# Causal and full attention heads on one core: other shapes of the head loads and of the bias path, a compact band, and zero-weight matmuls

## The chip, the core and the metric

The program runs on one core of one Trainium2 chip. The metric is the device time of one execution, in microseconds (us). Before the change three runs took 5108.78, 5110.0 and 5099.33 us (median 5108.78).

## What is computed

The input `x` is 2 x 2048 x 256, float32. It goes through two layers, each an attention and a feed-forward part:

```
x += attn0(LN(x))    16 heads of 16, all 2048 keys: softmax(q k^T) v, then Wff and a bias
x += moe(LN(x))      6 experts, top 2, and a shared one (also ahead of attn0: "macaron")
x += 0.5 * lstm(LN(x))
x += attn1(LN(x))    16 heads of 16, causal, rotary q and k, and a relative-position term:
                     scores[q,k] += q . rel[clip(k - q, -32, 32) + 32]
                     ctx[q]      += sum_k attn[q,k] rel[clip(k - q, -32, 32) + 32]
x += 0.5 * lstm(LN(x))
```

With two batches each attention has 32 heads (`NH`). In the causal one every key more than 32 back shares one row of `rel`, which is folded into the values. Only a band of 32 keys (`REL`) before each query needs a score term and an output term of its own.

## The kernel before, in words

The stages are, in order: `moe_stage` 0, `qkv_full_stage`, `heads_full_stage`, `project_full_stage`, `moe_stage` 1, `lstm_stage`, `qkv_causal_stage`, `heads_causal_stage`, `project_causal_stage`, `lstm_stage`. Each writes out one program per engine, and semaphores alone tie them together. SP issues nearly all transfers, in the order written, and a wait on SP holds back all behind it.

**Heads, both kinds.** q and k of a head lie in SBUF as 48 rows (high and low parts of float32r, 16 each) at partition 0 and again at 64, in a ring of four heads (`load`, L1126 to L1129 and L1495 to L1498). A 49th row of q is minus the row maximum (`row_load`, L1511), so that the score matmul (L1198, L1608) gives what exp takes. While PE scores head i, it also computes the maxima of heads i+1 and i+2 (`far`, L1226, L1659, L1665), and DVE reduces them. The order is written out in `body`: a causal head has 8 steps (`NSTEP`), each a pair of key tiles with five score matmuls, three `far` units, the bias added by matmuls with the identity (`bias`, L1619, L1622), and the weighted values (L1638) into bank 7. After the fifth step PE turns the maxima of head i+1 into a row (`row`, L1671), ACT copies it (L1740), and SP writes it into q of head i+1. The first score matmul of head i+1, in the last step of head i, waits for that.

**Bias path.** `qkv_causal_stage` leaves the 32 band scores of each query in DRAM (`rel_scores`, `k.TD`). `fill_bias_tiles` (called in `moe_stage` 1) has filled the array `bias_tiles` (`k.BB`) with 512 copies of a masked 128 x 160 tile. `skew(i)` (L1489) writes the 32 scores of each query over them, DRAM to DRAM, in runs of 128 bytes at a pitch of 161 numbers. Read back at a pitch of 160, each row is shifted by one more, which makes the diagonal band (`causal_bias`, L1502).

**Band path.** DVE adds the bias to the scores of the band, takes the maximum and leaves the sums in SBUF (L1794). POOL stores them to DRAM (`store_band`, L1571, `k.PB`). `project_causal_stage` reads the 32 band scores of each query back (`band`, L2002), in runs of 128 bytes.

**SP in a causal head** (`body` in `heads_causal_stage`): `load(i+3)`, which ends in the bias load and in `skew(i+4)`, then `store(i-1)`, then `row_load(i+1)`.

## Time and profile before

| | |
|---|---|
| three runs | 5108.78, 5110.0, 5099.33 us |
| the profiled execution | 5106.48 us, its span 5104.8 us, mean granted clock 0.888 |
| PE busy | 4455.2 us (87%) |
| DVE busy | 2996.9 us (59%) |
| ACT busy | 2297.0 us (45%) |
| POOL busy | 648.1 us (13%) |
| full heads, first load issued to last matmul | 640 to 2155 us |
| causal heads, first `skew` issued to last output copy | 3140 to 4728 us |
| projection of the causal heads | 4728 to 4873 us |

An engine's busy time is the sum of its instructions. The granted clock is TensorE's share of full speed: 1.00 is 2.4 GHz, 0.50 is 1.2 GHz. In a row of the timeline the first number is the start in us from the start of the span, the second the length. What stands in brackets is how long the engine was idle before, and what ended that. SPq is the queue of the sync engine.

### The profile page before, as it was taken

How to read it: one execution, taken by the hardware profiler on the slowest of the kernel's cores; microseconds unless marked ns; L12 is line 12 of the kernel's file. 1: busy time of each engine (PE TensorE's matmuls, PEld its weight loads, DVE VectorE, ACT ScalarE, POOL GpSimd, SP SyncE). 2: the span in 40 equal slices, each digit the busy share in tenths (PEclk: the TensorE clock that was granted, in tenths of full speed). 3: DMA queues.
4: the chain of work that ended last, by engine and by line, in shares of the span. 5: the costliest groups of instructions: out<-in, count | busy, mean ns of one | idle time of the engine just before them, and what ended most of it. 6: DMA issues, size and time to landing. Idle time of an engine off the chain costs nothing. (4 is left out here: it accounts for less than half of the span.)

```text
span 5104.8 us, 80050 instructions
## 1 busy us (share of the span) xinstructions
PE 4455.2 (87%) x25680; PEld 2625.2 (51%) x25680; DVE 2996.9 (59%) x5384; ACT 2297.0 (45%) x4375; POOL 648.1 (13%) x666
## 2 busy tenths in 40 slices
PE   7999859999999999889998965688978978889488
PEld 6888723333333333258886544345545545555355
DVE  6655668888888888456664355444444544444342
ACT  3222327777777777612222222334434434445222
POOL 2322100000000000013332024111111111111000
PEclk9999969999999999889999987778778878789699
DMA  2000311111111111039000026444444444341801
GB/s 77 0 0 1 138 50 42 42 39 41 37 37 42 42 38 33 11 113 296 0 0 18 0 86 183 112 93 93 103 95 95 105 94 96 97 98 44 133 26 33
DMA packets 316682, 343.08 MB, mean 67 GB/s; under 512 B 161280, under 2 KB 266760, under 8 KB 302600
## 3 DMA queue, kind: packets, MB, share of 16 engines
q1 hardware_dynamic: 299912, 296.20, 22.1%
q0 software_dynamic: 16384, 41.96, 2.9%
q8 instruction: 214, 3.51, 0.3%
q14 instruction: 172, 1.41, 0.1%
HBM read 239.26 MB, written 148.11 MB: 76 GB/s over the span
## 5 line engine op out<-in xcount | busy, mean ns | idle before, releaser
L1322 DVE TENSOR_REDUCE full_tops<-psum 128x1 f32<-128x1024 f32 x1024 | 1207.2, 1220 | 247.8 <-PE psum L1226 247.4
L1279 ACT ACTIVATE full_probs<-psum 128x512 f32<-128x512 f32 x2048 | 1067.2, 602 | 338.5 <-PE psum L1198 306.4
L1736 ACT ACTIVATE causal_probs<-psum 128x512 f32<-128x512 f32 (+3 forms) x1280 | 644.3, 533 | 761.2 <-PE psum L1622 389.4
L1784 DVE TENSOR_REDUCE causal_tops<-psum 128x1 f32<-128x1024 f32 (+7 forms) x704 | 587.4, 859 | 261.5 <-PE psum L1659 261.5
L1198 PE MATMUL psum<-full_q,full_k 49*128 49x512 f32 x2048 | 657.8, 482 | 49.5 <-ACT full_probs L1279 33.3
L1608 PE MATMUL psum<-causal_q,causal_k 49*128 49x512 f32 (+3 forms) x1280 | 465.3, 508 | 181.2 <-DMA causal_q<-causal_rows 171.0
L1198 PEld LDWEIGHTS psum<-full_q,full_k 49*128 49x128 f32 x2048 | 290.1, 189 | 640.4 <-ACT full_probs L1279 585.4
L1207 PE MATMUL psum<-full_probs,full_vh 128*32 128x512 f32 x4096 | 565.3, 625 | 0.7 <-ACT full_probs L1279 0.7
L1226 PE MATMUL psum<-full_k,full_q 48*128 48x512 f32 x2048 | 408.9, 463 | 64.7 <-DMA full_k<-qk_split 38.3
L1659 PE MATMUL psum<-causal_k,causal_q 48*128 48x512 f32 (+4 forms) x1152 | 375.2, 468 | 88.9 <-DMA causal_k<-rot_parts 46.9
L1638 PE MATMUL psum<-causal_probs,causal_vh 128*32 128x384 f32 (+3 forms) x3712 | 409.1, 501 | 1.2 <-ACT causal_probs L1736 1.2
L276 POOL TENSOR_TENSOR moe_h_lo<-moe_h,moe_h_hi 128x512 fp32r<-128x512 f32 x224 | 290.7, 1298 | 664.0 <-ACT moe_h_hi L389 664.0
L1608 PEld LDWEIGHTS psum<-causal_q,causal_k 49*128 49x128 f32 x1280 | 198.7, 212 | 320.7 <-DMA causal_q<-causal_rows 153.4
L313 PE MATMUL psum<-moe_x_hi,moe_w_hi 128*128 128x512 f32 x896 | 353.2, 394 | 3.9 <-DVE moe_h L455 3.8
L313 PE MATMUL psum<-moe_x_lo,moe_w_hi 128*128 128x512 f32 x896 | 350.9, 392 | 0.0
L313 PE MATMUL psum<-moe_x_hi,moe_w_lo 128*128 128x512 f32 x896 | 349.8, 390 | 0.0
L1794 DVE CUSTOM_DVE_ANT_0 xn<-psum,causal_bias 128x160 f32<-128x160 f32 (+1 forms) x384 | 107.5, 317 | 378.6 <-issue 378.6
L451 DVE TENSOR_TENSOR moe_ts<-psum,moe_sg 128x512 f32<-128x512 f32 x224 | 154.8, 691 | 296.8 <-ACT moe_sg L397 296.5
L1226 PEld LDWEIGHTS psum<-full_k,full_q 48*128 48x128 f32 x2048 | 203.8, 195 | 217.6 <-DVE full_tops L1322 153.6
L389 ACT CAST moe_h_hi<-moe_h 128x512 fp32r<-128x512 f32 x224 | 138.9, 620 | 384.5 <-DVE moe_h L455 384.5
L1619 PE MATMUL psum<-ident_sb,causal_bias 128*128 128x128 f32 x1024 | 285.6, 366 | 0.0
L1659 PEld LDWEIGHTS psum<-causal_k,causal_q 48*128 48x128 f32 x1152 | 216.8, 228 | 108.6 <-issue 41.7
(189 smaller groups left out, 6095.6 us busy)
## 6 DMA issues: line engine op xcount, KB each, us to landing
bias_tiles<-in_bias SPq DMA_DIRECT2D x4, 10240.0 KB, 86.5
causal_bias<-bias_tiles SPq DMA_DIRECT2D x32, 1280.0 KB, 27.7
band_scores<-xn POOLq DMA_DIRECT2D x192, 160.0 KB, 6.1
qk_split<-qkvf_parts SPq DMA_DIRECT2D x32, 512.0 KB, 3.4
full_q<-qk_split SPq DMA_DIRECT2D x64, 256.0 KB
full_k<-qk_split SPq DMA_DIRECT2D x64, 256.0 KB
rot_parts<-qkvc_parts SPq DMA_DIRECT2D x32, 512.0 KB, 3.1
causal_q<-rot_parts SPq DMA_DIRECT2D x64, 256.0 KB
```

Of the source, the lines that this page charges most:

```text
L276: nc.gpsimd.tensor_tensor(h_lo[:, r, u % C, :], hf[:, u % 2, :], h[:, r, u % C, :].bitcast(F32), ALU.subtract).then_inc(hl_ready, 1)
L313: last = nc.tensor.matmul(k.psum[:, 2 * (u % 2) + kind, :], W[wp][:, e, kind, c, m * P:(m + 1) * P], (xhi, xlo)[xp][:, half, c, :], start= ...
L1198: nc.tensor.matmul(k.psum[:, b, :], k_sb[at, q, kt * P:(kt + 1) * P], q_sb[at, q, n * BLK:(n + 1) * BLK], start=True, stop=True).then_inc( ...
L1207: last = nc.tensor.matmul(k.psum[32 * j:32 * j + VP, 7, :], vh[:, q % 2, kt, :], pT[:, kt % 4, j * BLK:(j + 1) * BLK], start=(kt == 0), st ...
L1226: last = nc.tensor.matmul(k.psum[:, b + c, :], q_sb[at, q, t * P:(t + 1) * P], k_sb[at, q, lo:lo + BLK], start=True, stop=True)
L1279: nc.scalar.activation(pT[:, kt % 4, n * BLK:(n + 1) * BLK], k.psum[:, bank(q, u), :], ACT.Exp).then_inc(p_ready, 1)
L1322: nc.vector.reduce_max(mx[:, q % 2, u // 2, u % 2:u % 2 + 1], src, AX_X).then_inc(m_free, 1)
L1608: last = nc.tensor.matmul(k.psum[:, b, 0:(hi - lo) * P], k_sb[at, q, kt * P:(kt + 1) * P], q_sb[at, q, lo * P:hi * P], start=True, stop=no ...
L1638: last = nc.tensor.matmul(k.psum[32 * j:32 * j + VP, 7, tiles[0] // QB * P:BLK], vh[:, q % 2, kt, :], pT[:, n % 2, first:first + QB * (len ...
L1659: last = nc.tensor.matmul(k.psum[:, b + side, at0:at0 + hi - lo], q_sb[at, q, t * P:(t + 1) * P], k_sb[at, q, lo:hi], start=True, stop=True)
L1736: nc.scalar.activation(dst, k.psum[:, bank(q, u), 0:(hi - lo) * P], ACT.Exp).then_inc(p_ready, 1)
L1784: last = nc.vector.reduce_max(mx[:, r, t, entry:entry + 1], both[:, off:off + hi - lo], AX_X)
```

## The change

Line numbers in this section are the changed kernel's.

1. **Head loads, both kinds.** Twelve loads of 16 rows take the place of eight loads, of which (causal) all, or (full) half, had 2 as the outermost size of their DRAM side. `rot_parts` is laid out with the head ahead of the halves, and is written by 8 stores a block for 4.
2. **Bias lines one longer.** `k.BB` now holds for each query one line of 16 x 160 numbers and one more. DVE puts 32 scores into each 160 of a masked line in SBUF (`spread`, half a head at a time), SP writes 128 lines of 5 KB to DRAM (`skew`), and reads them back at a pitch one shorter, 10 KB a row (`load_bias`). `fill_bias_tiles` is gone.
3. **SP reordered** (first order piece below): the store first, the row load behind the first `skew`, the bias load after it.
4. **Compact band.** POOL copies the 32 band scores of each query of a finished head, DRAM to DRAM, into `k.CD`, once a head (`compact_band`). The projection reads them in runs of 512 bytes, one transfer a block for four. The bands have 4 pairs of SBUF tiles for 8, so that DVE waits for the store of four steps before.
5. **Zero-weight matmuls.** In every step but the first of a head PE adds two matmuls with zero weights into bank 7, 256 columns each in bfloat16 (`keep_warm`).
6. **Small.** ACT copies the row ahead of two exps. Outputs and denominators of the causal heads go to one array with 4 stores a head for 8, from one buffer for two. `project_full_stage` reads the reciprocals broadcast by the load, in place of a matmul.

```diff
@@ heads_full_stage, SP: load
-    sp.dma_start(q_sb[base:base + 2 * DH, q, :].bitcast(F32), k.QF[0][0:2, row, :]).then_inc(qk_loaded[q], 16)
-    sp.dma_start(q_sb[base + 2 * DH:base + 3 * DH, q, :].bitcast(F32), k.QF[0][0, row, :]).then_inc(qk_loaded[q], 16)
-    sp.dma_start(k_sb[base:base + DH, q, :].bitcast(F32), k.QF[1][0, row, :]).then_inc(qk_loaded[q], 16)
-    sp.dma_start(k_sb[base + DH:base + 3 * DH, q, :].bitcast(F32), k.QF[1][0:2, row, :]).then_inc(qk_loaded[q], 16)
+    for x, tile, order in ((0, q_sb, (0, 1, 0)), (1, k_sb, (0, 0, 1))):
+        for j, part in enumerate(order):
+            dst = tile[base + j * DH:base + (j + 1) * DH, q, :].bitcast(F32)
+            sp.dma_start(dst, k.QF[x][part, row, :]).then_inc(qk_loaded[q], 16)
@@ heads_causal_stage, SP
+    def load_rel(i):
+        sp.wait_ge(spread_done, 2 * i)
+        sp.dma_start(compact[:, :, :], k.TD[bass.ds(i, 1), :, :, :].rearrange("a p t j -> p (a t) j")).then_inc(rel_loaded, 16)
+    def skew(i, part):
+        sp.wait_ge(spread_done, 2 * i + part + 1)
+        lines = k.BB[1:1 + NH * P * BIAS_ROW].rearrange("(h p x) -> h p x", h=NH, p=P)
+        dst = lines[bass.ds(i, 1), :, part * HALF_ROW:(part + 1) * HALF_ROW + part].rearrange("a p x -> (a p) x")
+        sp.dma_start(dst, skew_rows[:, 0:HALF_ROW + part]).then_inc(skewed, 16)
+    def load_bias(i, q):
+        heads = k.BB[0:NH * P * BIAS_ROW].rearrange("(h x) -> h x", h=NH)
+        src = heads[bass.ds(i, 1), 0:P * KT * BAND].rearrange("a (r t c) -> (a r) t c", r=P, c=BAND)
+        sp.dma_start(bt[:, q, :, :], src).then_inc(bt_loaded[q], 16)
...
-    def body(i, q):
-        load(i + 3, (q + 3) % 4)
-        store(i - 1, (q + 1) % 2)
-        row_load(i + 1, (q + 1) % 4)
+    def body(i, q, left):
+        store(i - 1)
+        sp.wait_ge(pv_done, (i + 3) * NSTEP + NSTEP)
+        load(i + 3, (q + 3) % 4)
+        skew(i + 4, 0)
+        sp.wait_ge(skewed, 32 * (i + 4))
+        row_load(i + 1, (q + 1) % 4)
+        load_bias(i + 3, (q + 3) % 4)
+        skew(i + 4, 1)
+        load_rel(i + 5)
@@ POOL
+    def compact_band(i, q):
+        for n in range(PAIRS, NSTEP):
+            pool.wait_ge(band_stored[n], 16 * (i + 1))
...
+        src = k.PB[bass.ds(i * KT, KT), 1:1 + P * SKEW].rearrange("t (r c) -> r t c", c=SKEW)[:, :, 0:REL]
+        dst = k.CD[bass.ds(i, 1), :, :, :].rearrange("a p t j -> p (a t) j")
+        pool.dma_start(dst, src).then_inc(k.compacted[q], 16)
@@ PE, in each step with n > 0, between far and bias
+    for side in range(2):
+        nc.tensor.matmul(k.psum[:, 7, 2 * side * P:2 * (side + 1) * P], zeros.bitcast(BF16), k.ident[:, :].bitcast(BF16),
+                         start=False, stop=False, skip_group_check=True)
@@ DVE
-    dve.wait_ge(band_stored[n], 16 * i)
+    if n >= PAIRS:
+        dve.wait_ge(band_stored[n - PAIRS], 16 * (i + 1))
+    elif not first:
+        dve.wait_ge(band_stored[n + PAIRS], 16 * i)
...
+    def spread(i, part):
+        if part == 0:
+            dve.wait_ge(rel_loaded, 16 * (i + 1))
+        dve.wait_ge(skewed, 16 * (2 * i + part))
+        nc.vector.memset(skew_rows[:, HALF_ROW:HALF_ROW + 1], 0.0)
+        wide = skew_rows[:, 0:HALF_ROW].rearrange("p (t c) -> p t c", c=BAND)
+        tiles = slice(part * KT // 2, (part + 1) * KT // 2)
+        nc.vector.tensor_copy(wide[:, :, 0:REL], compact[:, tiles, :]).then_inc(spread_done, 1)
@@ project_causal_stage, SP: band
-    for t in range(TB):
-        tile = bass.DynSlice(batch(n) * H * KT + within(n) * TB + t, H, KT)
-        src = k.PB[tile, 1:1 + P * SKEW].rearrange("h (r c) -> r h c", c=SKEW)[:, :, 0:REL]
-        sp.dma_start(wt[:, half, t, :].rearrange("p (h j) -> p h j", h=H), src).then_inc(s_wt[half], 16)
+    src = k.CD[bass.ds(batch(n) * H, H), :, bass.ds(within(n) * TB, TB), :].rearrange("h p t j -> p h (t j)")
+    sp.dma_start(wt[:, half, :, :, :].rearrange("p h t j -> p h (t j)"), src).then_inc(s_wt[half], 16)
```

`spread(i + 4, 0)` and `spread(i + 4, 1)` stand after the 12th and the 21st of DVE's 24 units of a head.

The issues of SP in the loop over causal heads, one head, before (`causal_rows` is the row of maxima, `out_heads` and `denominators` take the output):

```order
L1495 DMA causal_q<-rot_parts 32x1x2048
L1496 DMA causal_q<-rot_parts 16x1x2048
L1497 DMA causal_k<-rot_parts 16x1x2048
L1498 DMA causal_k<-rot_parts 32x1x2048
...
L1502 DMA causal_bias<-bias_tiles 128x16x160
L1489 DMA bias_tiles<-rel_scores 128x16x32
L1520 DMA out_heads<-causal_out 64x1x128
L1521 DMA denominators<-causal_out 4x1x128
...
L1511 DMA causal_q<-causal_rows 1x16x128 x2
L1512 DMA row_tops<-causal_top_short 128x16
```

And in the changed kernel:

```order
L1523 DMA causal_heads<-causal_out 128x1x128
...
L1507 DMA causal_q<-rot_parts 16x2048 x2
L1507 DMA causal_k<-rot_parts 16x2048 x3
L1507 DMA causal_q<-rot_parts 16x2048 x3
L1507 DMA causal_k<-rot_parts 16x2048 x3
L1494 DMA bias_tiles<-causal_skew_rows 128x1280
L1514 DMA causal_q<-causal_rows 1x16x128 x2
L1515 DMA row_tops<-causal_top_short 128x16
L1499 DMA causal_bias<-bias_tiles 128x2560
L1494 DMA bias_tiles<-causal_skew_rows 128x1281
L1488 DMA xn<-rel_scores 128x512
```

The row load no longer stands behind a DRAM-to-DRAM transfer of 128 x 16 runs, but behind the twelve loads and one write of 128 runs.

PE in the middle of a step of the changed kernel (`ident_sb,xn` is the zero-weight pair, its weights a part of `xn`):

```order
L1711 MATMUL psum<-causal_k,causal_q 128x160 x2
L1696 REGISTER_ALU
L1705 MATMUL psum<-causal_k,causal_q 128x512 x2
L1722 MATMUL psum<-ident_sb,xn 128x256 x2
L1665 MATMUL psum<-ident_sb,causal_bias 128x128
L1668 MATMUL psum<-ident_sb,causal_bias 32x32
```

The pair is new; what stands around it is as before.

## Rows read from the trace of the kernel before

**Rows 1.** The page, engines over the whole span.

```profile
PE 4455.2 (87%) x25680; PEld 2625.2 (51%) x25680; DVE 2996.9 (59%) x5384; ACT 2297.0 (45%) x4375; POOL 648.1 (13%) x666
```

**Rows 2.** Stretches: engines' busy us, PEclk, DMA share, GB/s.

```profile
3139.86:3241.42 101.56, 21.41 (x78) 11.23 (x79) 36.53 (x97) 0.26 (x1) 12.21 (x15) 0.50 0.49 114
3241.42:4727.52 1486.10, 1295.14 (x8626) 766.12 (x8626) 693.27 (x1958) 666.37 (x1343) 190.08 (x275) 0.80 0.39 93
...
4430.00:4456.00 26.00, 26.00 (x123) 14.46 (x119) 10.03 (x32) 9.42 (x19) 2.58 (x4) 0.51 0.19 60
4584.00:4622.00 38.00, 35.75 (x272) 21.72 (x272) 22.46 (x64) 20.87 (x42) 6.10 (x9) 0.94 0.41 116
```

**Rows 3.** Waits, the one for the row load.

```profile
PE psum L1608 <- DMA causal_q<-causal_rows: 171.0, 24, 25.0
```

**Rows 4.** Timeline of one causal head, PE and SPq.

```profile
3903.23 0.79 PE L1608 MATMUL psum<-causal_q,causal_k 49*128 49x512 f32 x1 [9.41 <-DMA causal_q<-causal_rows]
...
3910.00 1.11 PE L1608 MATMUL psum<-causal_q,causal_k 49*128 49x512 f32 x3
...
3917.31 20.85 SPq L1489 DMA_DIRECT2D bias_tiles<-rel_scores  x1
...
3917.44 1.01 PE L1608 MATMUL psum<-causal_q,causal_k 49*128 49x512 f32 x3
...
3929.76 0.73 PE L1608 MATMUL psum<-causal_q,causal_k 49*128 49x512 f32 x3
...
3933.87 0.67 PE L1608 MATMUL psum<-causal_q,causal_k 49*128 49x512 f32 x3
...
3939.90 0.50 PE L1659 MATMUL psum<-causal_k,causal_q 48*128 48x512 f32 x2 [1.12 <-ACT causal_rows L1740]
```

**Rows 5.** Timeline, ACT: copies of the row (L1740) and of the output (L1745).

```profile
4041.35 0.24 ACT L1740 CAST causal_rows<-psum 16x128 fp32r<-16x128 f32 x1
4053.96 0.59 ACT L1745 COPY causal_out<-psum 128x512 f32<-128x512 f32 x1 [0.92 <-PE psum L1638]
...
4242.90 0.59 ACT L1745 COPY causal_out<-psum 128x512 f32<-128x512 f32 x1 [0.92 <-PE psum L1638]
4265.25 0.24 ACT L1740 CAST causal_rows<-psum 16x128 fp32r<-16x128 f32 x1
...
4698.14 0.59 ACT L1745 COPY causal_out<-psum 128x512 f32<-128x512 f32 x1 [0.62 <-PE psum L1638]
4727.52 0.59 ACT L1745 COPY causal_out<-psum 128x512 f32<-128x512 f32 x1 [1.37 <-PE psum L1638]
```

**Rows 6.** Landing of the 32 transfers of L1489, and DMA issues of L1571.

```profile
DMA to landing us min/median/max: 8.3/29.2/30.4
...
band_scores<-xn POOLq DMA_DIRECT2D x192, 160.0 KB, 6.1
```

**Rows 7.** Timeline, PE: two matmuls of 256 columns in the first QKV stage.

```profile
620.56 0.28 PE L951 MATMUL psum<-qkvf_w_hi,qkvf_x_hi 128*128 128x256 f32 x1
620.68 0.28 PE L951 MATMUL psum<-qkvf_w_hi,qkvf_x_lo 128*128 128x256 f32 x1
```

**Rows 8.** Timeline, start of the full heads, and PE at a turn of their loop.

```profile
639.83 0.80 SPq L1126 DMA_DIRECT2D full_q<-qk_split  x1
...
670.25 1.22 PE L1226 MATMUL psum<-full_k,full_q 48*128 48x512 f32 x4 [38.31 <-DMA full_k<-qk_split]
...
897.92 0.62 PE L1198 MATMUL psum<-full_q,full_k 49*128 49x512 f32 x2 [2.09 <-issue]
```

**Rows 9.** Timeline of both projections: a PE row of the full one, DVE of the causal.

```profile
2207.38 1.98 PE L1912 MATMUL psum<-big 8*128 8x512 f32 x4
...
4771.57 2.50 DVE L2122 TENSOR_TENSOR proj_band<-proj_band,proj_tops 128x512 f32<-128x512 f32 x4 [16.31 <-DMA proj_band<-band_scores]
...
4797.47 2.50 DVE L2122 TENSOR_TENSOR proj_band<-proj_band,proj_tops 128x512 f32<-128x512 f32 x4 [1.43 <-DMA proj_band<-band_scores]
4810.53 2.50 DVE L2122 TENSOR_TENSOR proj_band<-proj_band,proj_tops 128x512 f32<-128x512 f32 x4 [1.52 <-DMA proj_band<-band_scores]
```

More of the change, by code:

```diff
@@ L1529, in _ @@
                 sp.wait_ge(ones, 4)
-                for q in range(3):
-                    load(q, q)
+                load(0, 0)
+                skew(0, 0)
+                skew(0, 1)
+                load_rel(1)
+                load(1, 1)
+                sp.wait_ge(skewed, 32)
+                sp.wait_ge(edge_set, 16)
+                load_bias(0, 0)
+                skew(1, 0)
+                skew(1, 1)
+                load_rel(2)
+                load(2, 2)
+                sp.wait_ge(skewed, 64)
@@ L1817, in _ @@
                         far(1, 1, p)
+                spread(3, 1)
                 def body(i, q, left):
-                    for ahead, h, p in segment(q, left):
+                    more = not isinstance(i, int) or i + 4 < NH
+                    for at, (ahead, h, p) in enumerate(segment(q, left)):
                         if p == 1 and ahead == 2:
@@ L1823, in body @@
                         far(i + ahead, h, p)
+                        if at in (11, 20) and more:
+                            spread(i + 4, at // 20)
                     if left == 1:
@@ L1867, in project_full_stage @@
     bias = take(D)
-    spread = take(P)
     s_w, s_rec, s_rc = sem("weights"), sem("recip_dma"), sem("recip")
     s_ld = [sem(f"loaded{r}") for r in range(2)]
-    rb_ready = sem("rb_ready")
     o_ready = sem("o_ready")
@@ L1908, in blockwise @@
             def blockwise(n, half, last):
-                pe.wait_ge(s_ld[half], 32 * (n // 2 + 1))
-                for c in range(C):
-                    pe.wait_ge(o_ready, 2 * C + (n - 1) * C + c + 1)
-                    nc.tensor.matmul(k.psum[:, c, :], spread[0:HC, :], rd[0:HC, half, c, :],
-                                     start=True, stop=True).then_inc(rb_ready, 1)
                 pe.wait_ge(o_ready, 2 * C + (n + 1) * C)
@@ L2154, in blockwise @@
                 def blockwise(n, half, left):
-                    if left > 1:
-                        lower(n + 2, half)
                     update(n)
@@ L2159, in blockwise @@
                         combine(n + 1, 1 - half)
+                    if left > 1:
+                        lower(n + 2, half)
                 looped_ahead(dve, NBLK, blockwise)
```

221 lines of the change are left out of this document (127 added, 94 removed).

## The prediction, made before the change was run

> **What bounds the kernel now.** I read the page first. PE is busy 87% of the span [rows 1], so a gain has to come from the time in which PE waits, or in which it runs at half clock. The table of stretches shows where that is. In the 1486.1 us of the causal heads PE is busy 1295.1 us at a mean granted clock of 0.80 [rows 2]. So two things are lost there: 191 us without a matmul, and the slow matmuls. In the list of waits the largest one of PE in this stage is the wait for the row load, 171.0 us in 24 heads [rows 3].
>
> The timeline of one head shows why [rows 4]. The transfer `bias_tiles<-rel_scores` (L1489) keeps SP for 20.85 us. The stores and the row load stand behind it, and PE waits 9.41 us for the row. Then PE runs cold. Score matmuls of one step to those of the next take 7.44 us (3910.00 to 3917.44) at 1.2 GHz, and 4.11 us (3929.76 to 3933.87) at 2.4 GHz. So a cold step costs 3.33 us more. A head took 1486.1/32 = 46.4 us on average [rows 2]. What a head takes without the wait and at full clock comes from two pairs of ACT rows [rows 5]: output copy to row copy 22.35 us, row copy to output copy 12.61 us, together 34.96 us. The last head, which has no maxima to make, took 29.4 us [rows 5]. After the row stall is gone, PE itself is the limit: in the 38 us after 4584, a stretch without that stall, PE is busy 35.75 us at clock 0.94 [rows 2].
>
> **The change, part by part.** The sum is made against the profiled span of 5104.8 us. Its execution took 5106.48 us, 1.7 more than the span, and 2.3 below the median of the runs.
>
> *The row load.* In the new order SP has ahead of it 4 stores, 12 loads and one write of bias lines. A load of q or k is issued in 0.80 us [rows 8], so 17 issues take about 14 us. The half `skew` waits for DVE's twelfth unit of 24, near step 4 of 8, some 17 us into the head. PE makes the row after the fifth step, and needs it loaded in the last one. So SP is ready at about 18 us, the row at about 22 (22.35 in [rows 5]), and the load is there well before the 29 us at which the last step starts. The stall goes, wholly. What is late next is PE's own work.
>
> *A causal head after.* I start from 34.96 us.
> - ACT copies the row at once, and no longer behind two exps. Before, PE waited 1.12 us for it [rows 4]. Take −1.0 (bounds −1.1 and 0).
> - Two matmuls of 256 columns in 7 steps: 14. Two of that width follow each other by 0.12 us [rows 7], at full clock, so +1.7. They cover the whole array and can't run beside the 48-row pairs around them. Lower bound 0, upper bound 0.24 each (half clock), +3.4.
> - Two `spread`s on DVE, of 256 numbers a partition each. A sum of 512 takes 2.50/4 = 0.63 us [rows 9], so about 0.3 each. DVE is busy 22.46 of 38 us in an unstalled head [rows 2], so most of it hides; +0.6 at most on the path, since PE's `far` waits for DVE with two slots. I take 0.6, lower bound 0.
> - What is left of the cold clock. In the full heads, where nothing stalls, PE still has a gap of 2.09 us once per turn of the loop over four heads [rows 8], and the clock falls behind it. The causal loop has the same turn. The gap and two cold steps are 2.1 + 6.7 = 8.8 us per four heads, 2.2 a head. The zero-weight matmuls may shorten that; I take 1.7 (bounds 0 and 6.7, two cold steps in each head).
>
> That is 38.0 us a head. 31 × 38.0 + 29.4 for the last + 5 for the cold start of the first = 1212 us, against 1486. **−274 us.**
>
> *Filling the causal stage.* From the first `skew` to the first score 101.6 us pass at clock 0.50 [rows 2], because three L1489 transfers of 20 us or more stand between the loads and ahead of the first row load. Now the loads of two heads (24 issues, 19 us) and small transfers stand ahead of the first bias load, which lands at about 30 us. Then DVE's maxima of one head and a half are the limit: 36.5 us busy in that stretch before [rows 2], with `spread`s and gaps some 46. 30 + 46 = 76. **−25** (−10 to −40).
>
> *The full heads.* The first load is issued at 639.83, and PE starts at 670.25, 30.4 us later [rows 8]. Half of these loads have 2 as outermost size. With 16 rows each the twelve issues take 5 to 8 us and the last one lands a few us later: 12 us. **−18** (−8 to −24). The steady full heads wait for no load, so four more issues a head cost nothing there: SP waits for PE and ACT most of the time. If that cover went, they would cost some 3 us a head.
>
> The Trainium skill, "DMA: Bandwidth & Descriptors", section "Why a DMA increments its semaphore by 16 and not by 1", says that a transfer runs on as many engines, up to 16, as divide the slowest dimension of both sides: 2 before, 16 now. No row here names the engines; the 30.4 us for the first head fit it.
>
> *The causal projection.* The band reaches DVE every 13.06 us (4797.47 to 4810.53), after a wait for its load each time [rows 9]. With runs four times as long and one transfer for four, the next limit is DVE, ACT and PE in turn; DVE's subtraction of 2.50 us, PE and the rest come to some 9.5 us a block. Six blocks × 3.5 = 21, and of the wait of 16.31 us for the second band [rows 9] most goes, 14. **−35** (0 to −50).
>
> *The full projection.* Four matmuls of 1.98 us in all go from each of 8 blocks [rows 9]. They lie mostly beside DVE's bias additions. **−4** (−16, all of them, to +5, since the reciprocals now come 16 times as wide).
>
> *At nothing.* The 40 MB that filled `bias_tiles` ran under the second mixture of experts, whose matmuls never waited for it. The 32 more stores in the causal QKV stage stand where SP waits for POOL.
>
> Sum: −274 − 25 − 18 − 35 − 4 = −356. 5104.8 − 356 + 1.7 = **4751 us**.
>
> **The rivals.**
>
> *A. The clock stays low without a stall.* From 4430 to 4456 PE was busy all 26.0 us, and the clock was 0.51 [rows 2]. So a full queue alone doesn't bring it back. If the zero-weight matmuls don't either, two cold steps a head stay: 6.7 in place of 1.7, 43.0 us a head, 4751 + 31 × 5 = **4906 us**. For it speaks that row; against it the 38 us after 4584 at 0.94.
>
> *B. The clock holds by itself.* PE no longer stops for more than a moment, so no head is cold: 38.0 − 1.7 = 36.3, 4751 − 31 × 1.7 = **4698 us**. In that case the zero-weight matmuls are pure cost, 1.7 × 31 = 53 us. The Trainium skill, "TensorE: Matmul & The Clock Gate", section "What's actually happening", says this: activity releases the throttle, and a busy PE runs warm. The row at 4430 speaks against it: PE busy without a gap, and cold.
>
> *C. The row load is still late.* SP's chain through DVE's `spread` (skew, wait, skew) or crowding of the loads keeps it back. Half of the old stall with its cold step, 3 + 3, a head: 4751 + 31 × 6 = **4937 us**. Then the change would not do what it says.
>
> *D. Slower: POOL's compaction holds up DVE.* It moves 2048 runs of 128 bytes from DRAM to DRAM, as L1489 did, and that took 29.2 us to land in the median, 8.3 us when nothing else was queued [rows 6]. The band stores stand behind it in POOL's queue, and need 6.1 us themselves [rows 6]. DVE may now be only four steps ahead of a store: 4 × 4.11 = 16.4 us. At 29.2 + 6.1 = 35.3 us it waits 19 us in each head, PE with it, and a cold step follows: 22.3 more than 38.0, 4751 + 31 × 22.3 = **5442 us**. It becomes slower than before when the two together land later than some 28 us. Against it: the slow landings of L1489 came while the loads of q and k held the queue, and the first one, alone, took 8.3; 8.3 + 6.1 = 14.4 is under 16.4. The Trainium skill, "DMA: Bandwidth & Descriptors", section "Specifications", gives 512 bytes as the least transfer for line rate, with a read-modify-write below it; the compaction is below it, as L1489 was.
>
> **How the numbers follow.** A measurement of this kernel can tell about 0.2%, 10 us, from no change. Chances: the forecast 0.50, A 0.24, B 0.12, C 0.08, D 0.06. The forecast, A and B hold 0.86. From 4660 (B, with 40 us for the bounds of the other terms) to 4915 (A, and a little) takes them in for the most part. Faster by over 0.2% are all but D and a small part of the unknown: 0.94; within 0.2% 0.01; slower 0.05.
>
> **What would show it.** In the profile of the changed kernel: PE's wait of [rows 3] near 0; output copies of the causal heads 38 us apart; granted clock of that stage above 0.93 (A: 0.85 or less); twelve loads of the first full head landed 12 us after the first issue; bands in the projection under 11 us apart; POOL's compaction landing in under 11 us, and no wait of DVE for `band_scores` (D: 19 us a head). The forecast is wrong if output copies are over 40 us apart, or if DVE or PE waits for a transfer in the steady heads.

## The result, and the profile after

The changed kernel takes 4773.77 us in the median of 4 runs (4765.35 to 4786.46), the kernel before 5108.02: a ratio of 0.9351, 95% interval 0.9327 to 0.9374. The forecast was 4751, range 4660 to 4915. The profiled execution has a span of 4763.8 us against 5104.8, 341 less, where the sum had 356 less.

The page's engines over the whole span, which answer to [rows 1]:

```profile
PE 4313.7 (91%) x26096; PEld 2571.5 (54%) x26096; DVE 3006.5 (63%) x5514; ACT 2299.2 (48%) x4375; POOL 683.2 (14%) x698
```

The stretch of the causal heads, first score to last output copy, with the columns of [rows 2]:

```profile
3205.32:4382.87 1177.55, 1150.05 (x9076) 706.00 (x9073) 705.20 (x2075) 667.26 (x1344) 226.52 (x309) 0.95 0.60 160
```

It was 1486.10 us at clock 0.80 with 191 us without a matmul; now 27.5 us are without one, at 0.95. The wait of [rows 3] is gone from the steady heads. All that PE waits for from 3250 to 4382.9 (us in total, times, longest; a releaser "issue" means that the engine waited for nothing that the profile shows):

```profile
PE psum L1654 <- issue: 13.1, 6, 2.8
PE psum L1654 <- ACT causal_probs L1789: 9.0, 8, 1.2
PE psum L1684 <- ACT causal_probs L1789: 0.8, 1, 0.8
```

ACT's copies of the output (L1798) and the row (L1793), to be read against [rows 5]:

```profile
3405.17 0.59 ACT L1798 COPY causal_out<-psum 128x512 f32<-128x512 f32 x1 [0.86 <-PE psum L1684]
3426.80 0.26 ACT L1793 CAST causal_rows<-psum 16x128 fp32r<-16x128 f32 x1 [0.88 <-PE psum L1717]
3439.76 0.59 ACT L1798 COPY causal_out<-psum 128x512 f32<-128x512 f32 x1 [0.86 <-PE psum L1684]
```

21.63 + 12.96 = 34.59 us, and this repeats to 0.1 us in two heads of four. In the third PE waits 1.25 us for an exp of ACT (seven of the eight waits in the second row above; its cause comes with the run that has PE, ACT, DVE and POOL written out). Some 7 us later comes the turn of the loop over four heads. The timeline of PE at one turn, and the stretch behind it:

```profile
3513.13 1.11 PE L1654 MATMUL psum<-causal_q,causal_k 49*128 49x512 f32 x3 [2.77 <-issue]
```
```profile
3513.00:3537.00 24.00, 23.87 (x104) 13.74 (x105) 8.50 (x24) 7.85 (x16) 2.58 (x4) 0.50 0.54 107
```

PE stops for 2.77 us (at the six turns 1.4 to 2.8 us), waiting for nothing that the profile shows, and is then busy for 23.87 of 24 us at half clock. The 31 heads between the first and the last output copy (3255.29 to 4382.87) average 36.4 us; without the last, which makes no maxima, 36.6.

By stage, in us of the two profiled executions: start of the program to the last output of the full heads, −18; full projection +1; second mixture of experts, first LSTM and causal QKV −3; filling of the causal stage −16.5 (101.6 to 85.1); causal heads −308.5; causal projection +1 (146.3 to 147.2); second LSTM +3. These make −341.

### The profile page after: what moved, and what is told of

Its sections match the earlier page's. It is cut to its first block and busy times, and to the rows that moved or that the text cites. A ratio compares the mean times of both kernels' runs of the same rounds, so it can differ in the third digit from the quotient of the medians.

```text
span 4763.8 us, 81796 instructions
## 1 busy us (share of the span) xinstructions
PE 4313.7 (91%) x26096; PEld 2571.5 (54%) x26096; DVE 3006.5 (63%) x5514; ACT 2299.2 (48%) x4375; POOL 683.2 (14%) x698
## 5 line engine op out<-in xcount | busy, mean ns | idle before, releaser
L1654 PE MATMUL psum<-causal_q,causal_k 49*128 49x512 f32 (+3 forms) x1280 | 412.6, 456 | 22.7 <-issue 13.1
L1705 PE MATMUL psum<-causal_k,causal_q 48*128 48x512 f32 (+4 forms) x1152 | 329.5, 419 | 68.6 <-DVE causal_tops L1856 32.3
L1684 PE MATMUL psum<-causal_probs,causal_vh 128*32 128x384 f32 (+3 forms) x3712 | 348.3, 438 | 0.8 <-ACT causal_probs L1789 0.8
L1607 POOL DMA_DIRECT2D band_scores<-xn x256 | 187.8, 733 | 892.2 <-DVE causal_tops L1856 888.1
L1856 DVE CUSTOM_DVE_ANT_0 xn<-psum,causal_bias 128x160 f32<-128x160 f32 (+1 forms) x512 | 143.5, 318 | 188.1 <-issue 188.1
L395 ACT ACTIVATE moe_sg<-psum 128x512 f32<-128x512 f32 x224 | 133.8, 597 | 260.6 <-PE psum L311 259.3
L325 PE MATMUL psum<-moe_w_hi,moe_h_hi 128*128 128x256 f32 x896 | 255.8, 286 | 2.5 <-POOL moe_h_lo L274 2.5
```

The lines of the kernel that those rows point to most:

```text
L1654: last = nc.tensor.matmul(k.psum[:, b, 0:(hi - lo) * P], k_sb[at, q, kt * P:(kt + 1) * P], q_sb[at, q, lo * P:hi * P], start=True, stop=no ...
L1684: last = nc.tensor.matmul(k.psum[32 * j:32 * j + VP, 7, tiles[0] // QB * P:BLK], vh[:, q % 2, kt, :], pT[:, n % 2, first:first + QB * (len ...
L1705: last = nc.tensor.matmul(k.psum[:, b + side, at0:at0 + hi - lo], q_sb[at, q, t * P:(t + 1) * P], k_sb[at, q, lo:hi], start=True, stop=True)
```

## The experiments

Where one execution stands for an edit, stages are compared. How far a stage of the same code moves by itself is seen in the causal heads of the kernel before: 1486.1, and 1469.2 in the run of the full heads' loads below, where nothing of this stage was edited. So less than some 20 us there says nothing. The causal projection of the kernel before took 145.6 to 152.1 us in the six runs that have it unedited (median 149.4), that of the changed kernel 143.3 to 146.6 in four (143.4). The full projection took 77.9 to 82.7 us over all runs. The full heads, from the first to the last output copy, took 1382.3 to 1406.8 us in the twelve runs in which their loops were not all written out.

### What made the stall

*Only the wide loads, in the kernel before* (layout, stores and loads of the causal q and k parts).

```
-    k.QC = [... (2, 2, NH, HALF, S) ...]
+    k.QC = [... (2, NH, 2, HALF, S) ...]
-        4 loads of a side of the array, two with outermost size 2
+        6 loads of a side, one part of 16 rows each; LOADS = 12
```

> The kernel before with the causal heads' q and k parts laid out, stored and loaded as in the changed kernel (16 rows as outermost size, 12 loads a head); all else as before. Kernel before: the transfer bias_tiles<-rel_scores keeps SP for some 20.85 us a head, PE waits 171 us in 24 heads for the row, causal heads 1486.1 us. Theory 1 (the loads of q and k, on few engines, stand in the queues ahead of that transfer, and its landing of 29.2 us is theirs): it lands in about 10 us, SP is held for a few us, the row wait goes, the stage falls to some 1250 to 1350 us. Theory 2 (the transfer's own 2048 runs of 128 bytes between DRAM and DRAM are slow wherever it stands): SP is still held for some 20 us, the row wait stays over 120 us, the stage within 30 us of 1486.

Measured: 4875.5 us; the causal heads 1254.9 us, 231 less. The transfer between two places in DRAM (here L1490), first its time on SP's queue (ns, min/median/max), then its landing:

```profile
L1490 SPq DMA_DIRECT2D bias_tiles<-rel_scores x32: 605/7244/9050, 3159.1 to 4314.5; - x32
...
DMA to landing us min/median/max: 9.5/19.1/22.1
```

The hold of SP fell from 21.2 to 7.2 us, the landing from 29.2 to 19.1, though the transfer is the same one. PE's wait for the row is 0.5 us in all from 3250 on. So these loads alone give 231 of the 308 us, though no wait of the profile before named them. They also shorten the filling, from the first `skew` to the first score: 73.2 us (3159.12 to 3232.30) against 101.6. Theory 1 holds, except that the landing was 19 and not 10 us: the transfer is slow by itself too.

*Only SP's order, in the kernel before.*

```
                 def body(i, q):
-                    load(i + 3, (q + 3) % 4)
                     store(i - 1, (q + 1) % 2)
                     row_load(i + 1, (q + 1) % 4)
+                    load(i + 3, (q + 3) % 4)
```

> The kernel before with one change, the order of SP in a causal head: store of the head before, row load, and only then the loads of q, k and bias of the head three ahead, with the write of bias lines (before: loads first). Theory 1 (the order alone makes the stall: the row stands behind the 20.85 us that SP is held): the row wait of 171 us goes to under 20 us; if the clock then holds by itself the stage is 31 x 36 = about 1130 to 1200 us, if it does not, 31 x 41 = about 1270 us. Theory 2 (the row load would be late anyway, for it shares the queues with slow loads, or these loads now come late themselves): PE still waits over 60 us in all for a row or for q and k, the stage over 1350 us.

Measured: 4993.5 us; the causal heads 1356.1 us, 130 less, clock 0.86. PE's first waits:

```profile
PE psum L1659 <- DMA causal_k<-rot_parts: 34.9, 7, 6.2
PE psum L1608 <- DMA causal_q<-causal_rows: 33.2, 8, 25.5
PE psum L1659 <- ACT causal_rows L1740: 32.3, 30, 1.1
```

Theory 2, in its second form: over 60 us of waits, and a stage over 1350. The row mostly came in time (of 33.2 us, 25.5 are the wait of the first head, at the end of the filling), but narrow loads issued later now came late themselves. The order alone is worth a little over half of what the loads are.

*The changed kernel with the narrow loads again* (all eight have 2 as outermost size, not four as the expectation has it).

```
-    k.QC = [... (2, NH, 2, HALF, S) ...]
+    k.QC = [... (2, 2, NH, HALF, S) ...]
-        6 loads of a side, one part of 16 rows each; LOADS = 12
+        4 loads of a side of the array, two with outermost size 2; LOADS = 8
```

> The changed kernel with the causal heads' q and k parts laid out, stored and loaded as before (outermost size 2 in four of eight loads a head); all else as changed. Changed kernel: causal heads 1177.6 us, PE waits for no load in a steady head. Theory 1 (narrow loads fill a few queues for 20 us or more, and whatever stands behind them is late: bias lines, spread rows, the row): PE or DVE wait for loads in most heads, the stage over 1250 us. Theory 2 (only the old transfer between two places in DRAM suffered behind them; the new, shorter chain of SP has slack enough): no wait of PE over 20 us in all, the stage within 20 us of 1177.6. In both the filling before the first score is longer than the 86 us of the changed kernel, by 10 to 20 us.

Measured: 4979.0 us; the causal heads 1354.9 us, 177 more. From 3250 on PE waits 79.3 us in 18 heads for the row, and DVE stands before a `spread`:

```profile
DVE causal_skew_rows L1878 <- issue: 105.8, 18, 20.4
```
```profile
bias_tiles<-causal_skew_rows SPq DMA_DIRECT2D x32, 640.0 KB, 16.7
```

This write of 640 KB lands in 16.7 us in the median; in the changed kernel it took 3.1. Theory 1 again: whatever is queued behind the narrow loads is late. The filling took 114.7 us from the first transfer of `bias_tiles` to the first score, against 83.2 in the changed kernel: 31 more, where 10 to 20 were expected. The whole change without the wide loads comes to about the same stage as the order alone. The row load put back behind the other loads, in the changed kernel, was not tried.

### Why the clock is at 1.00 now

*Without the zero-weight matmuls.*

```
-                        if n > 0:
-                            keep_warm()
```

> The changed kernel without its 14 zero-weight matmuls a head; nothing of the result is left out. Changed kernel: causal heads 1177.6 us, warm head 34.59 us (row copy to row copy), clock 1.00 between the turns of the loop. Theory 1 (the clock was low only because of the row stall; rival B of the prediction): the clock holds without them, a warm head is 14 x 0.12 = 1.7 us shorter, 32.9 us, the stage 31 x 1.7 = 53 us shorter, 1125 us, the kernel some 4720 us. Theory 2 (they hold the clock up; rival A): cold spells within the turns come back, a head takes 38 to 43 us, the stage 1230 to 1380 us, the kernel 4820 us or more.

Measured: 4743.9 us in the median of 4 (4739.78 to 4758.53), ratio to before 0.9299, interval 0.9256 to 0.9343. The causal heads:

```profile
3218.50:4367.65 1149.15, 1120.21 (x8628) 679.33 (x8626) 705.35 (x2075) 664.99 (x1343) 226.74 (x309) 0.95 0.62 164
```

The clock is the same 0.95, a warm head takes 33.7 us in place of 34.6, and the stage is 28.4 us shorter. So in the changed kernel the zero-weight matmuls hold nothing up; 0.9 us for 14 is 0.065 us each. Theory 1 had the mechanism; its 53 us were sized at twice the cost.

*With them, in the kernel before.*

> The kernel before with the two zero-weight matmuls in seven of eight steps of each causal head, and a memset for their weights; nothing else. The stall of some 9 us a head for the row stays. Theory 1 (they bring the clock back, or hold it, wherever PE has work): clock of the causal heads over 0.88 (before 0.80), stage shorter than 1486.1 by 50 us or more. Theory 2 (they are pure cost where the stall drops the clock anyway): clock 0.80 as before, stage 31 x 1.7 to 31 x 3.4 us longer, 1539 to 1592 us.

Measured: 5110.6 us; the causal heads 1471.0 us at clock 0.84, within the 20 us by which this stage moves. Neither theory's number: no gain in time that can be told, nor the loss of 53 us, which was sized at twice what they cost. The clock is above the 0.80 and 0.81 of the two runs that have this stage unedited. So behind long stalls the zero-weight matmuls may shorten the time at half clock by about what they cost; one run doesn't show it.

*ACT's copy of the row behind the two exps again*, zero-weight matmuls kept.

```
+                        exps(i, q, n, (3, 4))
                         if left and n == ROW_STEP + 1:
                             ...
                             row(i + 1, (q + 1) % 4)
-                        exps(i, q, n, (3, 4))
```

> The changed kernel with ACT's copy of the row behind the two exps again, as before. Theory 1 (PE's wait of 1.12 us for it comes back): PE shows some 30 waits of about 1.1 us for causal_rows, a warm head takes 35.6 to 36.0 us in place of 34.59. Theory 2 (PE has work in its queue that covers it, or the exps that come later cost as much as the row that comes earlier): within 0.3 us of 34.59.

Measured: 4863.9 us; the causal heads 1277.0 us at clock 0.90, **99 us more**, for waits that last 32.5 us (from 3250 on; one more comes before):

```profile
PE psum L1705 <- ACT causal_rows L1793: 32.5, 29, 1.1
```

PE's timeline at one of them, and the stretches from it on:

```profile
3643.60 0.49 PE L1705 MATMUL psum<-causal_k,causal_q 48*128 48x512 f32 x2 [1.12 <-ACT causal_rows L1793]
...
3646.56 2.36 PE L1684 MATMUL psum<-causal_probs,causal_vh 128*32 128x256 f32 x16
```
```profile
3641.80:3643.60 1.80, 0.68 (x8) 0.48 (x6) 0.58 (x5) 1.21 (x3) 0.00 (x0) 1.00 0.01 3
3643.60:3646.60 3.00, 3.00 (x21) 2.04 (x23) 1.22 (x1) 1.10 (x3) 0.73 (x1) 0.89 0.22 63
3646.60:3648.90 2.30, 2.30 (x19) 0.95 (x18) 1.09 (x2) 0.37 (x1) 0.00 (x0) 0.50 0.93 218
```

Here the clock falls to 0.50 2.3 us after PE has resumed (0.89 is the mean of the 3.00 us), with PE fully busy in between. The 16 weighted matmuls take 2.36 us; at full clock they take 1.28. The granted clock fell so behind 21 of the 30 waits, 1.2 to 2.9 us after PE had resumed; behind nine it held. With the wide loads in the kernel before it fell behind 20 of 30. Theory 1 was right on the wait (warm heads of 35.9) and missed the clock: heads of 37.4 and 41 us, 3.2 us a head on average. The zero-weight matmuls, running here, did not prevent it.

*The kernel before with both edits, wide loads and the row copy first.* The first diff above, and:

```
-                        exps(i, q, n, (3, 4))
                         if left and n == ROW_STEP + 1:
                             ...
                             row(i + 1, (q + 1) % 4)
+                        exps(i, q, n, (3, 4))
```

> The kernel before with the wide q and k loads of the causal heads and, beside them, ACT's copy of the row ahead of the two exps of its step; nothing else of the change. With the wide loads alone the causal heads took 1254.9 us, 36.5 us in most heads, PE waiting 1.1 us for the row copy in 30 of them. Putting the copy behind the exps in the changed kernel cost 100 us (1277.4 against 1177.6), not the 31 us that the waits themselves last: the clock fell behind each wait. Theory 1 (these two edits are all that the causal heads gained): no waits for causal_rows, heads of 33.7 us between the turns, the stage 1150 to 1165 us. Theory 2 (SP's order, the bias lines and the compact band add to it): 1190 us or more.

Measured: 4781.8 us; the causal heads 1173.6 us at clock 0.93, two heads of four at 33.7 to 34.9 us. That is 9 us over theory 1's range and below theory 2's: two edits, the loads and one line of ACT's order, give the causal heads what the whole change gives (1177.6), and the kernel all but 8 us of it (4773.8). The whole change, however, pays 28 us for the zero-weight matmuls. Against the changed kernel without them (1149.2), SP's order, the bias lines and the compact band together are worth 24 us at most, little more than the stage moves by itself.

### The other stages

*Only the loads of the full heads, in the kernel before.*

```
-        dma_start(q_sb[base:base + 2 * DH, ...], k.QF[0][0:2, row, :])
-        ... 4 loads of a side
+        for j, part in enumerate(order):
+            dma_start(tile[base + j * DH:base + (j + 1) * DH, ...], k.QF[x][part, row, :])
```

> The kernel before with only the loads of the full heads changed (12 of 16 rows each in place of 8). Theory 1: the first head's load falls from 30.4 us to about 15 us, everything behind it comes 16 to 18 us earlier, the steady full heads are the same, and the kernel is 16 us faster, some 5093 us. Theory 2 (the steady heads gain too, since later loads no longer crowd the row load; or lose by four more issues): the full stage changes by over 25 us or by under 8.

Measured: 5082.1 us. The first head's issue to PE's first maxima, 636.33 to 650.92:

```profile
650.92 1.22 PE L1226 MATMUL psum<-full_k,full_q 48*128 48x512 f32 x4 [22.47 <-DMA full_k<-qk_split]
```

14.6 us, against 30.4 [rows 8]; theory 1 for the load. The steady full heads didn't change (42.5 us between turns), but the last output came only 9 us earlier than before, not 16 to 18: the last head took 64.4 us in place of 46.4. The clock fell to 0.50 at 2079 in this run and at 2141 before. Why it falls at different times in the last heads is open.

*The causal projection with the band from* `band_scores` *again, and DVE and ACT in the order of before*, in the changed kernel.

```
-                    src = k.CD[...]
-                    sp.dma_start(wt[...], src).then_inc(s_wt[half], 16)
+                    for t in range(TB):
+                        src = k.PB[tile, 1:1 + P * SKEW]....[:, :, 0:REL]
+                        sp.dma_start(wt[:, half, :, t, :], src).then_inc(s_wt[half], 16)
-                    compact_band(i, q)
```

The order of DVE and ACT is that of the next diff.

> The changed kernel with POOL's compaction and the compact band taken out: the causal projection reads the band from band_scores in four loads a block, in runs of 128 bytes, as before, with DVE's and ACT's order of before too; everything else as changed. Beside the run with the compact band and the old order (u3) it shows what the compact band is worth. Theory 1 (the many short runs set the pace: DMA share was 0.89 to 0.99 in this stage before): bands 13 us apart, stage some 146 us. Theory 2 (DVE, ACT and PE set it): bands 10 to 11 us apart, stage some 125 us. In the heads theory 1 of the compaction being free says no change over 5 us; if it slows other transfers, the causal heads are over 10 us shorter than 1177.6.

Measured: 4796.7 us; the causal heads 1184.0 us, 6 from 1177.6: no cost of the compaction can be told.

*The compact band kept, the same old order; and PE's heads written out*, without zero-weight matmuls.

```
 DVE
+                    if left > 1:
+                        lower(n + 2, half)
                     update(n)
                     if left > 0:
                         combine(n + 1, 1 - half)
-                    if left > 1:
-                        lower(n + 2, half)
 ACT
                     for t in range(TB):
                         copy(n + 1, t)
+                        exp(n + 2, half, t)
-                    for t in range(TB):
-                        exp(n + 2, half, t)
 PE, both head stages
-                full_heads_loop(pe, body)
+                for i in range(NH):
+                    body(i, i % 4, min(NH - 1 - i, 2))
```

> The changed kernel with three edits, each in a stage of its own: no zero-weight matmuls (as in the run without them); PE's program for the heads written out 32 times in place of a loop over four heads (both head stages; the other engines keep their loops); and in the causal projection DVE and ACT in the order of before (subtraction for block n+2 first, copies and exps alternating). Nothing of the result is left out. Theory 1 (a turn of PE's loop stops it for 2.1 to 2.8 us, the clock falls behind it, and 8 to 24 cold us follow): without turns all heads are warm, output copies of the full heads 42.4 us apart throughout (now 44.6 on average), those of the causal heads 33.7, so -60 us on the full heads and -50 on the causal ones against the run without zero-weight matmuls. Theory 2 (the stop comes with any long program, from the fetching of instructions, or the clock falls by itself every 150 us or so): the stops stay, both stages within 15 us. For the projection, theory 1 (its new order is what makes a serial chain of DVE, ACT and PE in 13.9 us a block): blocks fall to 10 to 11 us, stage 147 to some 125 us. Theory 2 (PE with its bank changes is the limit anyway): 13 us or more a block, within 8 us of 147. All together by the first theories: some 4610 us.

Measured, last output copy of the heads to the last update of the projection: before 146; changed 147; compact band with the old order 140; band from `band_scores` with the old order 157. So the compact band is worth 17 us. The new order costs 3 to 7: the changed kernel's stage is 143.3 to 146.6 in four runs, and with the old order it is 140.0 here and 139.4 in the last run below. The 157 is 5 to 11 us over the 146 to 152 of the code before, and this came with the rest of the change: numerators in two loads from `causal_heads` for one, and the band kept in SBUF with the heads outermost and its exps in a tile of their own. Neither was tried by itself. In the changed kernel's timeline the new order reads as a chain:

```profile
4454.43 2.49 DVE L2202 TENSOR_TENSOR proj_band<-proj_band,proj_tops 128x512 f32<-128x512 f32 x4
4455.15 2.44 ACT L2166 ACTIVATE proj_band_exp<-proj_band 128x512 f32<-128x512 f32 x4 [8.51 <-DVE proj_band L2202]
4455.83 1.97 PE L2120 MATMUL psum<-ident_sb,proj_band_exp 128*128 128x128 f32 x8 [3.26 <-ACT proj_band_exp L2166]
4463.04 0.69 DVE L2218 TENSOR_TENSOR X<-psum,X 128x512 f32 x1 [6.12 <-PE psum L2141]
```

The subtraction starts the exp, the exp the transposes, and the update waits behind them for PE; 13.9 us a block (4454.43 to 4468.32). With the old order the bands come 12.7 us apart, not 10 to 11, for DVE now waits up to 4.1 us for the band's load: neither theory had that.

PE's loop written out changed nothing in the heads (full heads as before, causal heads 1150 us). ACT's timeline at the same place of the loop says why:

```profile
3379.22 1.47 ACT L1792 ACTIVATE causal_probs<-psum 128x512 f32<-128x512 f32 x3 [2.07 <-issue]
```
```profile
3379.88 0.58 PE L1659 MATMUL psum<-causal_q,causal_k 49*128 49x256 f32 x1 [1.87 <-ACT causal_probs L1792]
```

PE had no turn any more, but ACT had, and PE waited for it. The kernel took 4745.2 us (ratio 0.9294, 0.9265 to 0.9323): the two theories were put on the wrong engine.

*PE, ACT, DVE and POOL all written out*, and in the projection an earlier band load.

```
-                full_heads_loop(act, body)
+                for i in range(NH):
+                    body(i, i % 4, min(NH - 1 - i, 2))
 ...
                 def band(n, half):
-                    sp.wait_ge(tp_ready, (n + 1) * TB)
+                    if n >= 2:
+                        sp.wait_ge(exp_done, (n - 1) * TB)
```

> The changed kernel without the zero-weight matmuls, with the programs of PE, ACT, DVE and POOL for the heads written out 32 times (SP keeps its loop) in both head stages; nothing of the result is left out. Writing out PE's alone left a stop every four heads: ACT stood 2.07 us and DVE 2.45 us with no releaser at the turn of their own loops. Theory 1 (the turns of the loops of all engines are the only cause of the stops): no cold spell in the steady heads, output copies of the full heads 42.4 apart throughout and of the causal heads 33.7, the causal heads 31 x 33.7 + 29 + some 25 at the start = 1100 us (1150.4 with PE's alone written out), the full heads 60 us shorter, the kernel some 4635 us. Theory 2 (some of the stops are fetching of instructions that no form of the program avoids): spells remain, under half of the 110 us is gained. In the causal projection DVE and ACT have the order of before, and the band load for block n+2 waits for the exps of block n only, no longer for its transposes. Theory 1 there (the load's start and landing of 8.6 us set the pace): bands from 12.7 us apart on average to 10.5 to 11.5, the stage 8 to 13 us shorter than 140. Theory 2 (the loads of num and recip ahead of it on SP set it): unchanged within 3 us.

Measured: **4641.9 us** in the median of 4 (4634.24 to 4647.13), ratio to before 0.9083, interval 0.9037 to 0.9128. The causal heads:

```profile
3159.40:4264.82 1105.42, 1090.68 (x8630) 665.71 (x8628) 701.74 (x2075) 667.17 (x1344) 227.08 (x309) 0.98 0.65 170
```

Output copies are 33.7 us apart, with 35.2 every fourth. From the first to the last output copy the full heads take 1340.8 us, against 1382.3 in the changed kernel and 1396.5 and 1399.6 in the two runs before this without zero-weight matmuls, and are warm throughout from 716 to 2024. A stop every four heads remains:

```profile
3306.24 1.09 ACT L1792 ACTIVATE causal_probs<-psum 128x512 f32<-128x512 f32 x2 [0.91 <-PE psum L1659]
...
3307.42 0.47 PE L1659 MATMUL psum<-causal_q,causal_k 49*128 49x512 f32 x1 [1.22 <-issue]
```

It isn't a rest of the turn. The changed kernel has it too, 7 us ahead of each turn, and there the profile names what ended it:

```profile
3356.43 0.49 PE L1654 MATMUL psum<-causal_q,causal_k 49*128 49x512 f32 x1 [1.25 <-ACT causal_probs L1789]
```

The code says why. Score unit u of a head in slot q of the ring goes to bank 4 + (q + u) mod 3 (`bank`), and a head has 40 units. So from one head to the next the rotation over three banks goes on, except where q goes from 3 back to 0: unit 39 and the next head's unit 0 both get bank 4. There PE has to wait for ACT's exp of the unit just scored. The two exps above end at 3307.33, PE goes on at 3307.42, and all seven stops of both runs show the same distance of about 0.1 us. It costs 1.5 us in four heads. A rotation that goes on across the ring wasn't tried.

The clock outlived this wait in five of seven cases; after those at 3988.65 and 4130.70 it fell. In the changed kernel it had fallen behind three of the six (3804.92, 3951.57 and 4097.91) before the turn came. So there the turn isn't the sole cause of the cold spell. Which of ACT, DVE and POOL had to be written out besides PE wasn't tried. The earlier band load gained nothing (143 us; theory 2).

*Another filling.*

```
-                load(1, 1)
                 sp.wait_ge(skewed, 32)
                 ...
                 load_bias(0, 0)
                 skew(1, 0)
                 skew(1, 1)
                 load_rel(2)
-                load(2, 2)
+                load(1, 1)
 ...
                 row_load(0, 0)
-                load(3, 3)
+                load(2, 2)
                 skew(3, 0)
                 skew(3, 1)
+                load(3, 3)
```

> The run with PE, ACT, DVE and POOL written out, with two edits more, neither in the steady heads. In the filling of the causal stage SP issues the q and k loads of head 1 behind the first bias load and both bias writes of head 1, those of head 2 behind the first row load, and those of head 3 behind the bias writes of head 3. Before that DVE stood 17.02 us for the first bias tile and 11.22 us for a bias write that was queued behind twelve loads. Theory 1 (the twelve loads ahead of them in the queues are what makes them late): the first bias tile lands some 6 us earlier, the 11.22 us go to 3 or less, and from the first load of bias_tiles to the first score it takes some 70 us in place of 84.6. Theory 2 (DVE's maxima at half clock and PE's, not the transfers, set it): within 4 us of 84.6. In the projection the band load waits for the transposes again: 140 us (the earlier wait gave 143). The kernel some 4625 us by theory 1.

Measured: 4640.8 us (4636.21 to 4646.31), ratio 0.9099, 0.9071 to 0.9127: the same as the run before it. The filling fell from 85.0 to 73.6 us (3067.50 to 3141.10), nearly as theory 1 said. All of it came from the first bias tile, for which DVE waited 6.98 us; the wait for a bias write was still 10.38 us, where 3 or less was expected. But the causal heads took 22 us more: the first of them ran at a mean clock of 0.65, and the clock fell behind the bank wait at 3295.42, 3440.73 and 3578.51 as well, where the run before held it. The gain was given back; one profile doesn't tell whether by the edit or by chance.

## Why the prediction was right, step by step

**The row load.** Right that the stall goes wholly. What held SP was given as the order with its slow transfer; the runs put the larger part on the narrow loads (−231 us alone) and the smaller on the order (−130 alone). They are not additive: 231 and 130 are more than the 308 of the whole change.

**A causal head after** was put at 38.0 us; the 30 between the first and the last took 36.6 on average.
- The 1.0 us for ACT's row copy is right as a length (35.9 less 34.6 is 1.3) and wrong as a price. The step took the wait for its own length, though cold steps were priced in another line. It costs 3.2 us a head with the clock that falls behind it. The error didn't show in the sum, for the 34.96 us that I started from is a warm head with that wait (35.9 − 0.9 = 35.0), and the forecast took the cold steps from elsewhere.
- Zero-weight matmuls: 1.7 us taken, 0.9 measured: 0.065 each where the 0.12 of [rows 7] was taken.
- `spread`: 0.6 taken, about 0 measured; a warm head without the zero-weight matmuls is 33.7 = 34.96 − 1.3.
- Cold clock: 1.7 taken; 36.6 − 34.6 = 2.0 measured. It lies around the turns alone, as the step said, but 0.4 of it is the bank wait (1.5 us in four heads), which the step didn't have.

30 heads × 1.4 = 42 us less than forecast; the first head took 50.0 us (3205.32 to 3255.29), 7 more than the 43 of the sum. **−274 became −308.5.**

**Rival A** (two cold steps stay in each head) didn't come, but its mechanism is what the row copy behind the exps shows: 1277 us. **Rival B** (the clock holds by itself, the zero-weight matmuls are pure cost) was right that the zero-weight matmuls are pure cost in this kernel, at 28 us and not 53, and wrong that no head is cold: the clock fell around each of the six turns. The rule of the Trainium skill, "TensorE: Matmul & The Clock Gate", section "What's actually happening", that a busy PE runs warm, agrees with the heads at 1.00 between the turns, and not with the 24 us at 0.50 from 3513, in which PE was busy for 23.87. **Rivals C** and **D** didn't come. D's turning point, "later than some 28 us", left out the cold step that D itself counts: 356 us over 31 heads are 11.5, and 16.4 + 11.5 − 3.3 = 24.6 us. POOL's compaction landed in 5.3 us in the median, the band stores in 4.0, and DVE never waited for them:

```profile
DMA to landing us min/median/max: 4.2/5.3/10.5
```

**Filling:** −25 forecast, −16.5 measured. The step that failed is "the first bias load … lands at about 30 us": DVE had the first bias tile at 3160.5, 40 us after the start of the filling (3120.2), after a wait of 17.67 us. What came behind it took 45 us, where the step had 46, though 11.15 of them were a wait for a bias write. The wide loads alone, in the kernel before, gave −28 here, so the new bias path cost some 12 us of what they gained.

**Full heads' first load:** −18 forecast. 30.4 us became 14.7, not 12. That the last output also came 18 us earlier is partly luck: the same loads by themselves brought it 9 us earlier, and the stage moves by more than 20. These times and the wide loads in the causal heads agree with the section of "DMA: Bandwidth & Descriptors" of the Trainium skill cited there, on the engines of a transfer; no row here names the engines.

**Causal projection:** −35 forecast, +1 measured; this is the wrong term of the sum. The step said "the next limit is DVE, ACT and PE in turn; 9.5 us a block". They are in turn, but in series, since the change also moves `lower` behind `combine` and the exps behind the copies. I had not costed that reordering. A gain of 17 us from the band stands against losses of 3 to 7 for the order and 5 to 11 for the rest. Over the runs with the same code the stage gained 6 us (median 149.4 to 143.4). The sign "bands under 11 us apart" failed at 13.9.

**Full projection:** −4 forecast, +1 measured, inside its bounds, but the stage moves by 5 us from run to run, so neither can be told from nothing. **At nothing:** right for the second mixture of experts, which took 512.7 and 512.6 us from PE's first matmul to its last; it and the next two stages together came to −3.

The total was close by luck: the heads gained 34 us more than the step had and the projection, the filling and the full projection 49 less. The mechanism of the largest term, the row stall, was right.

## What to carry to other kernels

A wait has two prices: its length, and what PE's clock loses behind it. Here waits of 1.1 us cost 3.2 us each on average, so short waits of a full PE are worth more than the list of waits shows; try to remove them before adding work to keep the clock up. When a transfer is slow, look at what stands before it in the queues. Of the hold of 21 us, 14 belonged to loads that no wait named. When a stop repeats with a loop, write out all the engines that turn there: one alone hides the gain, since the next engine takes its place. And where buffers rotate inside a ring of another length, look at the place where the ring closes.

## What the runs showed of the hardware

- Behind 21 of 30 waits of 1.12 us without a matmul the granted clock fell to 0.50, 1.2 to 2.9 us after PE was busy again. Without that wait it stayed at 1.00 for some 130 us, from turn to turn, and with PE, ACT, DVE and POOL written out for 806 us (3184 to 3990).
- Once low in the changed kernel's steady heads, it stayed low for 3.4 to 23.9 us with PE busy for 90 to 100% of the time. Zero-weight matmuls of 128 rows hardly shortened that there: cold spells between 3280 and 4300 add up to 89 us with them and 96 without. In the kernel before they add up to 348 us with them, and to 420 and 406 in the two runs without.
- At the turn of the loop over four causal heads PE stood for 1.4 to 2.8 us; with PE's loop alone written out ACT stood there for 2.07 and DVE for 2.45 us. With the clock behind it the turns were about 100 us of this kernel (4743.9 to 4641.9; 56 of them in the full heads, 44 in the causal ones).
- The same DRAM-to-DRAM transfer landed in 29.2 us behind narrow loads and in 19.1 behind wide ones; a write of 640 KB in 16.7 and in 3.1.
